# Filler products on TensorE, and a new order of the first and the last stage, in a hybrid convolution, attention and FFN block

## What is computed

```python
x = x + conv_mixer(layernorm(x))    # rmsnorm, in_w, two depthwise convolutions, gate, out_w, residual
x = x + ffn(layernorm(x))           # ternary weights, low-rank addition, relu squared, projection
x = x + attention(layernorm(x))     # 16 heads of 8 channels, softmax over 1024 tokens
x = x + ffn(layernorm(x))           # the same weights as the first FFN
```

```python
def ffn(x):
    h = bitlinear(x, w_fc) + gate * (x @ v.T @ fast_b.T @ u.T)   # 128 -> 512
    return bitlinear(relu(h) ** 2, w_proj)                       # 512 -> 128
```

## Time and profile before

| | |
|---|---|
| median of 3 runs | 528.9 us (528.67 to 528.9) |
| the profiled execution | 530.41 us, its span 528.6 us |
| PE, DVE, ACT busy | 498.6, 438.3, 358.3 us |
| mean granted TensorE clock | 0.971 of full speed |

### The profile page before, as it was taken

The page is one execution under the profiler, slowest core; times in us unless marked ns, Lnnn a source line. Parts: engine busy times, 40 slices in busy tenths (PEclk is TensorE's granted clock), DMA queues, the critical chain, the costliest instruction groups (busy, mean ns, idle before and its releaser), DMA issues.

```text
span 528.6 us, 10281 instructions
## 1 busy us (share of the span) xinstructions
PE 498.6 (94%) x4118; PEld 228.3 (43%) x4118; DVE 438.3 (83%) x654; ACT 358.3 (68%) x691; POOL 70.2 (13%) x89
## 2 busy tenths in 40 slices
PE   4999999998799999999999999999999999998897
PEld 2454566765333333333333333333333333332576
DVE  5699149948897999999999999999999999921953
ACT  2726214354117888888888888888888888888431
POOL 4399930000010001001001000000000000000000
PEclk9999999999757999999999999999999999999899
DMA  8100000053400202003002002101100000000001
GB/s 209 42 2 2 1 9 1 1 208 110 151 10 1 70 15 81 2 2 82 2 1 75 11 1 53 31 1 42 42 2 2 2 2 3 1 1 2 0 21 60
DMA packets 14110, 17.96 MB, mean 34 GB/s; under 512 B 3600, under 2 KB 10175, under 8 KB 13551
## 3 DMA queue, kind: packets, MB, share of 16 engines
q1 hardware_dynamic: 13036, 16.58, 10.7%
q0 software_dynamic: 240, 0.46, 0.5%
q10 hardware_dynamic: 786, 0.27, 0.2%
HBM read 11.70 MB, written 5.24 MB: 32 GB/s over the span
## 4 chain that ended last, share of the span: by engine, by line
PE 82%; DVE 8%; ACT 5%; DMA 2%; issue 1%; SPq 1%; ACTq 0%; DVEq 0%
PE ps L1344 31%; PE ps L1395 26%; PE ps L1137 6%; PE ps L1127 6%; DVE mx L995 4%; PE ps L1148 2%; ACT gate L739 2%; PE ps L1362 2%; PE ps L1173 1%; PE ps L1159 1%; PE ps L1184 1%; PE ps L1114 1%; PE ps L1320 1%; ACT acc L739 1%; DMA x<-in_L_attn_a_x 1%
## 5 line engine op out<-in xcount | busy, mean ns | idle before, releaser
L995 DVE TENSOR_REDUCE mx<-ps 128x1 f32<-128x1024 f32 x256 | 312.8, 1225 | 15.9 <-PE ps L1344 13.8
L1344 PE MATMUL ps<-kt,qt 62*128 62x512 f32 x512 | 195.1, 464 | 7.1 <-DVE mx L995 4.1
L1362 PE MATMUL ps<-qt,kt 64*128 64x512 f32 x512 | 184.3, 452 | 0.8 <-ACT gate L739 0.7
L739 ACT ACTIVATE acc<-ps 128x512 f32<-128x512 f32 x256 | 138.6, 603 | 26.6 <-PE ps L1362 21.8
L739 ACT ACTIVATE gate<-ps 128x512 f32<-128x512 f32 x256 | 138.5, 604 | 15.7 <-PE ps L1362 12.7
L1344 PEld LDWEIGHTS ps<-kt,qt 62*128 62x128 f32 x512 | 80.0, 193 | 110.2 <-DVE mx L995 79.1
L1395 PE MATMUL ps<-gate,val 128*32 128x256 f32 (+1 forms) x976 | 81.4, 405 | 3.8 <-ACT gate L739 3.8
L1395 PE MATMUL ps<-acc,val 128*32 128x256 f32 (+1 forms) x976 | 80.5, 402 | 0.9 <-ACT acc L739 0.9
L1362 PEld LDWEIGHTS ps<-qt,kt 64*128 64x128 f32 x512 | 75.8, 186 | 12.5 <-ACT gate L739 6.4
L498 POOL TENSOR_TENSOR nm_s<-nm,nm_s 16x128 f32<-16x128 f32 x16 | 7.6, 477 | 266.3 <-ACT nm L717 266.3
L1395 PEld LDWEIGHTS ps<-gate,val 128*32 128x32 f32 x976 | 19.3, 108 | 47.2 <-issue 23.5
(11 more groups left out here) (182 smaller groups left out, 369.3 us busy)
## 6 DMA issues: line engine op xcount, KB each, us to landing
qt<-q_scr SPq DMA_DIRECT2D x64, 64.0 KB
kt<-k_scr SPq DMA_DIRECT2D x32, 128.0 KB
x<-in_L_attn_a_x SPq DMA_DIRECT2D x4, 256.0 KB, 5.6
q_scr<-attn SPq DMA_DIRECT2D x4, 256.0 KB, 2.2
k_scr<-attn SPq DMA_DIRECT2D x4, 256.0 KB, 2.4
q_scr<-gate SPq DMA_DIRECT2D x4, 256.0 KB, 2.1
k_scr<-gate SPq DMA_DIRECT2D x4, 256.0 KB, 2.3
qt<-nm_s SPq DMA_DIRECT2D x64, 4.0 KB
```

The lines of the kernel that those rows point to most:

```text
L739: act.activation(pexp[step % NPB][:, j, :], bank(e_bank(slot)), ACT.Exp, scale=SCALE).then_inc(e_read, 1)
L995: dve.tensor_reduce(mx[:, item % 2, at:at + 1], pair(lo), AX.X, ALU.max).then_inc(m_read, 1)
L1344: mm = pe.matmul(bank(m_banks(M_UNIT[u])[keys]), qt[r][rows, half, jj, c * P:(c + 1) * P], kt[r][rows, jj, keys, :], start=True, stop=True)
L1362: pe.matmul(bank(e_bank(slot)), kt[r][rows, jj, s // TC, s % TC * P:(s % TC + 1) * P], qt[r][rows, half, jj, :], start=True, stop=True).th ...
```

## The change

1. Start, PE: 7 filler products (`keep_busy`) of 128 columns before the first weights, and 8 more after their transposes. They write bank 5, and nothing reads them.
2. Start, order: `first_std(1)` goes ahead of the copy of the vector columns on ACT; the turns of chunks 2 and 3 on PE go from behind the eighth `in_wide(0, at)` to behind the sixth, and their two copies on ACT from behind the eighth `sent_in(0, at)` to behind the fourth.
3. Lead, PE: two filler products of 96 columns after each of units 6 to 21.
4. ACT: one Exp of a single column, unread, after `negate(0)`.
5. Tail, ACT: `stds(3, 0)` and `stds(3, 1)` go ahead of the last `copy_o`. DVE: `norm(3, 0)` goes ahead of the last `norm_o`. PE: the turn of chunk 0, `fc(0)` and the turn of chunk 1 go ahead of `project(2)` and `project(3)`, and the order of the rest changes as below.

```diff
@@ ScalarE, first stage
             turn_copy(TURN_MIX + 1)
+            first_std(1)
             ev(4, vcol[:, :], bank(7)[:, 0:NVEC])
             act.wait_ge(setup_ev, 4)
             for at in range(4):
                 sent_in(0, at)
-            first_std(1)
+            turn_copy(TURN_MIX + 2)
+            turn_copy(TURN_MIX + 3)
             for at in range(4, 8):
                 sent_in(0, at)
-            turn_copy(TURN_MIX + 2)
-            turn_copy(TURN_MIX + 3)
@@ ScalarE, attention and tail
             negate(0)
+            act.activation(warm[:, :], ident[:, 0:1], ACT.Exp)
...
-            copy_o(NQ - 1)
             stds(3, 0)
             stds(3, 1)
+            copy_o(NQ - 1)
             turn_copy(TURN_F2)
+            rectify(0, WIDE_F2, KH * NCH)
+            turn_copy(TURN_F2 + 1)
+            rectify(1, WIDE_F2, KH * NCH, 0, 2)
             stds(3, 2)
-            turn_copy(TURN_F2 + 1)
+            rectify(1, WIDE_F2, KH * NCH, 2, KH)
             stds(3, 3)
-            for c in range(NCH):
-                rectify(c, WIDE_F2, KH * NCH)
-                if c + 2 < NCH:
-                    turn_copy(TURN_F2 + c + 2)
+            turn_copy(TURN_F2 + 2)
+            rectify(2, WIDE_F2, KH * NCH)
+            turn_copy(TURN_F2 + 3)
+            rectify(3, WIDE_F2, KH * NCH)
@@ VectorE, tail
             projected(1)
+            norm(3, 0)
             norm_o(NQ - 1)
...
-            norm(3, 0)
             norm(3, 1)
+            squares(0, WIDE_F2, TOK_F2)
             projected(2)
+            squares(1, WIDE_F2, TOK_F2, 0, 2)
             projected(3)
             norm(3, 2)
-            squares(0, WIDE_F2, TOK_F2)
+            squares(1, WIDE_F2, TOK_F2, 2, KH)
             norm(3, 3)
             for c in range(NCH):
-                if c + 1 < NCH:
-                    squares(c + 1, WIDE_F2, TOK_F2)
                 take_tokens(TOK_F2, c)
+                if c + 2 < NCH:
+                    squares(c + 2, WIDE_F2, TOK_F2)
@@ TensorE
+            def keep_busy(b, n, cols):
+                for _ in range(n):
+                    pe.matmul(bank(b)[:, 0:cols], ident[:, :], ident[:, 0:cols], start=True, stop=True)
+
             pe.wait_ge(ident_ready, 1)
+            keep_busy(IDLE_BANK, 7, P)
             pe.wait_ge(s_w_in, 16)
...
             mm.then_inc(setup_mm, 1)
+            keep_busy(IDLE_BANK, 8, P)
             pe.wait_ge(s_w_fold, 16 * 3)
...
-            for at in range(2, len(IN_ORDER)):
+            for at in range(2, 6):
                 in_wide(0, at)
             turn_h(0, TURN_MIX + 2)
             turn_h(0, TURN_MIX + 3)
+            for at in range(6, len(IN_ORDER)):
+                in_wide(0, at)
...
                 unit(u)
+                keep_busy(O_BANK, 2, P * 3 // 4)
...
             turn_o(NQ - 1)
+            turn_h(3, TURN_F2)
+            fc(0, TURN_F2, WIDE_F2)
+            turn_h(3, TURN_F2 + 1)
             project(2)
-            turn_h(3, TURN_F2)
             project(3)
-            turn_h(3, TURN_F2 + 1)
-            fc(0, TURN_F2, WIDE_F2)
-            for c in range(NCH):
-                if c + 2 < NCH:
-                    turn_h(3, TURN_F2 + c + 2)
-                if c + 1 < NCH:
-                    fc(c + 1, TURN_F2, WIDE_F2)
-                proj(c, KH * NCH, TOK_F2)
+            fc(1, TURN_F2, WIDE_F2)
+            proj(0, KH * NCH, TOK_F2)
+            turn_h(3, TURN_F2 + 2)
+            fc(2, TURN_F2, WIDE_F2)
+            turn_h(3, TURN_F2 + 3)
+            proj(1, KH * NCH, TOK_F2)
+            fc(3, TURN_F2, WIDE_F2)
+            proj(2, KH * NCH, TOK_F2)
+            proj(3, KH * NCH, TOK_F2)
```

More of the change, by code:

```diff
@@ L62 @@
 O_BANK = 2
+IDLE_BANK = 5
 MBANKS = ((4, 5), (6, 7))
@@ L256, in build @@
         nm = sb("nm", [HT, P])
+        warm = sb("warm", [P, 1])
         nm_s = sb("nm_s", [HT, PARTS, P])
```

## The result

The changed kernel takes 544.99 us (median of 4 runs, 542.8 to 549.06) against 528.9: the recorded ratio is 1.029, with a 95% interval of 1.026 to 1.033. It is 16 us slower, where 1.2% faster was forecast. The ratios leave out executions over 1.5% above the fastest of the same kernel: three of twelve of the last candidate and five of the kernel before.

What follows compares the result with a forecast made beforehand. PE was busy 90% or more nearly everywhere, DVE paced the lead, and low PE clock cost time. Profiled 530.4 - 1.9 (start) - 2.7 (lead) - 1.5 (tail) = 524.3; median 1.5 lower, 522.8 us; range 521.0 to 526.8.

Steps and rivals of the forecast that it cites:

- The step that failed: Lead: if the clock still falls at its start, 2 or 3 units run at half clock, costing up to 1 us.
- The price of a filler: Lead: a filler pair takes 0.34 to 0.46 us at full clock, hidden under DVE's 1.23; 0.72 to 0.96 at half clock.
- Rival (d): Lead stays at half clock throughout, fillers a pure price: 16 units of 1.8 against 1.27, +8.5 us, 532.8 total; chance 0.05.
- The table preload: Lead: an early Exp takes ACT's table load out of DVE's first wait, saving about 1.2 us.
- rival c: Lead: the clock hunts between half and full, about 1.46 us a unit, 3.7 us worse than forecast, 526.5; chance 0.10.
- the 2.7 forecast: Lead: of 3.4 us DVE idle, 0.3 stays and 0.4 is allowed for a clock fall, leaving a gain of 2.7.
- The start: Start: fillers give full clock by 8.8, so the second batch's wides begin at 21.2 instead of 23.10, gaining 1.9 us.
- The tail: Tail: the new order starts fc(0) at 491.4 and ends PE at 523.8 instead of 525.3, gaining 1.5 us.
- The 1.1 us named: Whole kernel: 0.2%, 1.1 us, is what a measurement can tell from no change; faster was given 0.93.

Runs made afterwards that it cites:

- the last candidate: Changed kernel plus 7 fillers in PE's wait ahead of unit 6 and 7 in the tail's holes, keeping two of 96 columns per lead unit: 524.97 us, 0.992.

## Why the prediction was wrong

- **The step that failed** is in the lead: "If the fall still happens at the lead's start, 2 or 3 units run at half clock before it recovers, up to 1". The fall happened where the text had put it (at PE's wait of 1.69 us, with fillers only after unit 6), in the changed kernel and in all eight further profiles with that wait unfilled: by the 1 us windows, between 0.3 us before the wait's end and 2.0 us behind it. With the change's fillers behind it, it did not recover in 16 units. The cost of that was not up to 1 but 15.7 us.
- **Why I took it to recover:** I read PE's busy share as what brings the clock back ("PE would be dense in it"). The kernel before already spoke against that: 13.93 of 15 us busy at 0.50, and I had used that row only to say who paces. The Trainium skill (TensorE: Matmul & The Clock Gate, What's actually happening) says that activity releases the throttle; by busy time the trace disagrees, with 30.00 of 30 us busy at 0.50. The profile with the burst agrees, so I take it that the activity meant is not what the busy column shows.
- **The price of a filler** was mis-sized as well. At half clock the pair takes 1.10 in the chain and the unit 1.15: 2.25 where 1.8 to 2.0 was said. At full clock a unit with its pair takes 1.27, where "at most 1.19" was said, so they were never fully hidden: DVE's dense 1.23 is not reached. And 1.23 is no floor for DVE either: bare units at full clock started 1.13 us apart (137.38 and 138.51, filled hole without fillers).
- **Rival (d)** had it right in mechanism, with 0.05, and put it at 532.8: 8.5 us of price in place of 15.7 (1.8 a unit in place of 2.25) is most of the rest. The table preload is 1.2 more of it, and the median another 3.7: it was taken as 1.5 below the profiled time and lay 2.2 above it (544.99 against 542.80). It did not hunt (rival c): in every profile without the burst the clock, once down in the lead, stayed down until scores and `pv` came.
- **The table preload** (1.2 in the sum) was worth nothing while the clock stayed low behind it. With the clock up, preload and clock together gave 2.6 of the 2.7 forecast (346.1 against 348.7 us, one profile); no run parts the two.
- **The start** was right where it acts: -1.9 forecast, -1.7 measured at the second batch's wides, and the claim that the order alone brings nothing. **The tail** was right where it acts: -1.5 forecast, -1.4 measured, with the hole ahead of `fc(2)` in its place, though the list of where it comes from (1.0, 0.3, 0.5 and about 1, less 0.7) adds up to 2.1. That either arrives at the end is shown only for all parts without the fillers together (2.6 of 3.1); each alone is within the noise.
- The 1.1 us named as what a measurement can tell from none was too fine for single runs of this kernel: on three chips the kernel before spans 528.2 to 532.5 (21 runs), 528.0 to 536.1 (19) and 528.2 to 537.6 (29).

## What to carry to other kernels

Filler work for the clock has to act before the clock falls, so look for the idle stretch at which it falls and fill that one; fillers interleaved afterwards with work that runs at the low clock are paid at half clock and can turn the engine into the bound. Price them at half clock and ask for the worst case first: here they win some 1 us or lose 15 to 23. And PE's busy column did not tell whether the clock would return; a stretch of the same kernel that was busy at 0.50 was the better witness. Of what was run, the change without the lead's fillers (0.995, 0.992 to 0.998) beats both kernels without that risk, and so does the filled hole alone (0.996, 0.994 to 0.998). The filled hole with the fillers (0.992) is faster where its clock stays up, but the last candidate lost its clock in the same lead in at least three of twelve executions, and with them its mean is only 1.1 us below that of the kernel before.

## What was not expected of the hardware

- PE reads as busy 29.8 to 30.0 of 30 us while its clock stays at half for more than 30 us, with the identity or dense operands, narrow or wide; in one of two executions 32 records of 128 columns back to back, begun at 138.45, ended it after some 6 us (144 to 145).
- Whether the clock falls at a given wait differs between executions of one program (at 120 to 131 in three of fourteen profiles; in the lead with the hole filled and two fillers in at least three of 19 executions). At 120 to 131 it moved the lead's start by 1.7 to 3.5 us. What exactly decides it stays open; no run here took it apart.
- DVE's maxima (1.21 to 1.23 us each by the records) came one every 1.14 us over nine of them (10.27 us) in the run with one filler, so the 1.23 that I took for DVE's floor is not one. I have not tested why.

```profile
135.56 10.27 DVE L1001 TENSOR_REDUCE mx<-ps 128x1 f32<-128x1024 f32 x9 [0.99 <-PE ps L1361]
```
